# Splitting the second layer's first expert weights on ScalarE and GpSimd instead of VectorE

## The reference

```python
x = x + tanh(g_xattn[0]) * L0_xattn(layernorm(x), ctx)
x = x + tanh(g_ffn[0])   * L0_ffn(layernorm(x))
x = x + tanh(g_xattn[1]) * L1_xattn(layernorm(x), ctx, mask)
x = x + tanh(g_ffn[1])   * L1_ffn(layernorm(x))
# L1_ffn: the token rows are sorted by expert, cut into 8 equal chunks, and chunk e is worked by expert e
h = gelu(einsum('ecd,edf->ecf', chunks, w1)); y = einsum('ecf,efd->ecd', h, w2)
```

## Time and profile before

| | |
|---|---|
| median of three runs | 760.68 us (760.11 to 762.44) |
| profiled execution | 758.21 us, its span 756.4 us |
| mean granted PE clock of the profiled execution | 0.827 |
| busy in the span | PE 545.8, DVE 416.9, POOL 339.5, ACT 237.2 us |

### The profile page before, as it was taken

The page is one execution under the profiler, slowest core; times in us unless marked ns, Lnnn a source line. Parts: engine busy times, 40 slices in busy tenths (PEclk is TensorE's granted clock), DMA queues, the critical chain, the costliest instruction groups (busy, mean ns, idle before and its releaser), DMA issues.

```text
span 756.4 us, 17521 instructions
## 1 busy us (share of the span) xinstructions
PE 545.8 (72%) x5484; PEld 428.4 (57%) x5485; DVE 416.9 (55%) x1454; ACT 237.2 (31%) x415; POOL 339.5 (45%) x424
## 2 busy tenths in 40 slices
PE   1576755524799999991898897777871388999950
PEld 1333443401499899980454575666651166989950
DVE  4787697986033333334995377778568612222215
ACT  0321022121144444443422364554541021323210
POOL 6202107777255666666400000070747676666650
PEclk9886867656899999996689899696655599999985
DMA  7911001143132222343754264352324123322219
GB/s 205 270 36 43 29 1 53 51 136 109 50 81 79 75 82 73 81 130 120 210 169 142 54 179 123 109 161 50 71 63 131 46 55 101 85 78 77 71 58 311
DMA packets 73196, 76.54 MB, mean 101 GB/s; under 512 B 12984, under 2 KB 61368, under 8 KB 73064
## 3 DMA queue, kind: packets, MB, share of 16 engines
q1 hardware_dynamic: 58504, 50.98, 24.6%
q0 software_dynamic: 10224, 22.40, 9.5%
q10 hardware_dynamic: 4400, 2.26, 1.0%
HBM read 46.15 MB, written 29.34 MB: 100 GB/s over the span
## 4 chain that ended last, share of the span: by engine, by line
PE 51%; DVE 23%; POOL 8%; issue 8%; DMA 6%; ACT 1%; SPq 1%; POOLq 0%; DVEq 0%
PE PS L758 46%; POOL xs L517 5%; DMA work<-ys 3%; DVE stats L1331 3%; DVE XN L1352 2%; PE PS L947 2%; DVE X L1326 2%; DVE work L1741 2%; DVE work L1326 2%; DVE rtmp L1326 1%; POOL work L565 1%; DVE mv L1334 1%; PE PS L1097 1%; DVE nwt L1326 1%; POOL work L572 1%
## 5 line engine op out<-in xcount | busy, mean ns | idle before, releaser
L517 POOL DMA_INDIRECT xs<-pack,adr_i x80 | 78.0, 975 | 196.7 <-ACT pack L1172 141.1
L528 POOL DMA_INDIRECT ys<-work x144 | 140.7, 977 | 34.5 <-issue 34.5
L758 PE MATMUL PS<-w,work 128*128 x1152 | 144.3, 279 | 3.0 <-issue 2.2
L758 PEld LDWEIGHTS PS<-w,work 128*128 128x128 f32 x1152 | 135.3, 193 | 9.2 <-issue 7.1
L758 PE MATMUL PS<-work,w1h 128*128 128x256 f16 x576 | 99.8, 275 | 2.6 <-issue 1.3
L1224 ACT ACTIVATE work<-PS,b 128x256 f32<-128x256 f32 x160 | 62.6, 474 | 95.4 <-PE PS L758 95.4
L1326 DVE TENSOR_TENSOR work<-PS,work 128x256 f32<-128x256 f32 (+3 forms) x82 | 33.0, 404 | 94.4 <-issue 52.9
L758 PE MATMUL PS<-work,w1l 128*128 128x256 f16 x288 | 79.4, 276 | 0.0
L758 PE MATMUL PS<-work 97*64 97x256 f16 (+5 forms) x608 | 61.3, 316 | 16.2 <-DVE work L1458 9.4
L758 PE MATMUL PS<-ones 128*128 128x512 f16 x195 | 51.9, 426 | 27.8 <-DVE rows_i L1588 12.6
L1661 DVE TENSOR_SCALAR work<-PS,work 128x128 f32<-128x128 f32 x64 | 19.5, 346 | 79.1 <-PE PS L758 79.1
(11 more groups left out here) (262 smaller groups left out, 852.5 us busy)
## 6 DMA issues: line engine op xcount, KB each, us to landing
work<-xs SPq DMA_DIRECT2D x132, 65.0 KB
work<-ys SPq DMA_DIRECT2D x12, 512.0 KB, 6.0
k_parts<-work SPq DMA_DIRECT2D x24, 128.0 KB, 2.0
w<-k_parts SPq DMA_DIRECT2D x8, 384.0 KB
work<-k_parts SPq DMA_DIRECT2D x32, 96.0 KB
work<-q_parts SPq DMA_DIRECT2D x8, 384.0 KB
work<-q_parts SPq DMA_DIRECT2D x32, 96.0 KB
ys<-work POOLq DMA_INDIRECT x144
```

Of the source, the lines that this page charges most:

```text
L517: g.indirect_dma_start(xs[l], bass.IndirectOffsetOnAxis(adr_i[:, k, T:T + 1], 0), pack_of(l, c)[:, s, k, :].bitcast(U32), None)\
L528: g.indirect_dma_start(ys[l], bass.IndirectOffsetOnAxis(xin[:, q, u, :].bitcast(U32)[:, D:D + 1], 0), yrow[:, q, u, :], None).then_inc(ff[ ...
L758: return t.matmul(o, lhsT, rhs, start=start, stop=stop, skip_group_check=True)
```

## The change

VectorE's splits of the second layer are taken out. In the same iterations 3, 7, ... 31, ScalarE, behind its copy of the turned heads and ahead of its routing steps, scales the loaded weights in place (f32 to f32), waits for that, and copies them to float16 as the high part. GpSimd subtracts the high from the scaled weights: for experts 0 to 3 ahead of all scatters, for 4 and 5 ahead of chunk 2's scatters, for 6 and 7 ahead of chunk 4's. The waits that stood before the first split (the stores of the queries, which share the memory of `w1h` and `w1l`) move to ScalarE with it.

```diff
--- before.py
+++ after.py
@@ -291,6 +291,7 @@
         w2_in = sem("w2_in")
         pack_hi, pack_lo = sem("pack_hi"), sem("pack_lo")
         w1_lo = [sem(f"w1_lo{l}") for l in range(2)]
+        w1_scaled, w1_hi = sem("w1_scaled"), sem("w1_hi")
 
         ff = {k: [sem(f"f_{k}{u}") for u in range(n)] for k, n in
               (("xin", XS_LEAD), ("xT", 2), ("xT_sb", 2), ("up", 2), ("hid", 2), ("y", 2), ("yrow", 2), ("turn", 1),
@@ -549,7 +550,17 @@
                 rows, s_, value = y_slot(0, c)
                 pool.wait_ge(s_, value)
                 g.tensor_tensor(rows[:, :, 0, :], rows[:, :, 0, :], rows[:, :, 1, :], ALU.add).then_inc(y_sum, 1)
+            def low_w1(e):
+                pool.wait_ge(w1_hi, e + 1)
+                o = slice(e * FF, (e + 1) * FF)
+                g.tensor_tensor(w1l[:, o], w1raw1[:, e % 2, :], w1h[:, o], ALU.subtract).then_inc(w1_lo[1], 1)
+
+            for e in range(E // 2):
+                low_w1(e)
             for c in range(NC):
+                if c in (2, 4):
+                    for e in (E // 2 + c - 2, E // 2 + c - 1):
+                        low_w1(e)
                 if c < NC // 2:
                     for s in range(CT_TILES):
                         scatter(1, c, (s,))
@@ -1300,6 +1311,15 @@
                         act.wait_ge(q_blank, 1)
                         act.wait_ge(n_out, 32)
                         max_loaded(act, 0)
+                k = chunk_at(g, 3)
+                if k == 0:
+                    for c in range(NC):
+                        act.wait_ge(q_out[c], Q_STORED)
+                if k is not None:
+                    act.wait_ge(w1_in[1][k % 2], 16 * (k // 2 + 1))
+                    a.activation(w1raw1[:, k % 2, :], w1raw1[:, k % 2, :], ACT.Copy, scale=WSCALE).then_inc(w1_scaled, 1)
+                    act.wait_ge(w1_scaled, k + 1)
+                    a.activation(w1h[:, k * FF:(k + 1) * FF], w1raw1[:, k % 2, :], ACT.Copy).then_inc(w1_hi, 1)
                 for k in route_at("exp", g):
                     route_exp(1, k)
                 for c in route_at("high", g):
@@ -1762,12 +1782,6 @@
                     route_weights(1, k)
                 for c in route_at("pack", g):
                     route_pack(1, c)
-                k = chunk_at(g, 3)
-                if k == 0:
-                    for c in range(NC):
-                        dve.wait_ge(q_out[c], Q_STORED)
-                if k is not None:
-                    split_w1(1, w1raw1, k)
             route_table(1)
             experts(1)
             for c in range(NC):
```

## The result

The changed kernel took 765.88 us (median of 20 runs, 761.02 to 772.62) against 757.86 us (20 runs, 752.13 to 763.93) for the kernel before on the same chip: a ratio of 1.0104, with a 95% interval of 1.0079 to 1.0129. The forecast was +7.9 us, 1.0%.

What follows compares the result with a forecast made beforehand. GpSimd's scatter queue was taken to set the end from 559.93 us, the PE/VectorE loop before. Terms -2.1 + 1.5 + 3.3 and +5.2 gave +7.9: 766.1, with 2.5 carried over 768.6 us; range 763.4 to 771.0.

Steps and rivals of the forecast that it cites:

- partial port waits: Band of 763 to 767 us, where VectorE is held by GpSimd only in part; chance 0.27.
- the 2.5 us carried over: Earlier median of 760.68 us lies 2.5 above the profiled execution of 758.21; added to 766.1 to give 768.6.
- Queue on GpSimd, +5.2: Eighth subtraction, waiting for ScalarE, delays chunk 4's first of 32 back-to-back scatters: +5.2 us, bounds 4.8 and 6.0.
- VectorE's port, +3.3: GpSimd's subtractions 3, 4 and 5 hold VectorE's routing instructions at the shared SBUF port, 3 x 1.1 us; bounds 0 and 4.8.
- Number 4: GpSimd subtraction, counted from 0, behind chunk 1's last scatter: holds VectorE 1.1 us, felt at PE's 0.70 us wait at 514.71.
- number 6: GpSimd subtraction, counted from 0, on VectorE's normalisation at 550: no cost, 3.40 us of VectorE idle behind it.
- ScalarE's stalls, +1.5: ScalarE's pair delays PE after iterations 3 (+0.9 us) and 7 (+0.6), nothing elsewhere; bounds 0 and 4.
- VectorE's relief, -2.1: Splits removed from VectorE count only after iterations 15 and 23, 2 x 1.06 us; PE's clock 0 to 2.0 more, taken as 0.
- Rival 1: VectorE's port is not felt, routing instructions slip between: +4.6 us, 765.3 us; with partial port waits chance 0.27.
- Rival 2: VectorE's relief counts in full and PE's clock holds, no ScalarE stall or port wait: +1.1 us, 761.8 us; chance 0.07.
- Rival 3: VectorE's routing, not GpSimd's scatters, ends last, so the delay is absorbed: faster, 756.6 to 758.6 us; chance 0.06.
- Rival 4: Eighth subtraction is not waited for, only the loop's +2.7 us is left: 763.4 us; given no chance of its own.

Runs made afterwards that it cites:

- experiment 2: Changed kernel with the eighth split whole back on VectorE: 759.55 us, 1.0027 to the kernel before.
- experiment 4: Changed kernel with GpSimd's subtractions 3, 4 and 5 (counted from 0) each later, behind scatters of the next chunk: 761.50 us, 1.0047 to the kernel before.
- experiment 6: Changed kernel with subtractions 3, 4, 5 later behind scatters and the eighth split back on VectorE: 755.35 us, 0.9956 to the kernel before.
- Experiment 5: Changed kernel with the splits of experts 0 and 1 back on VectorE: 765.56 us, 1.0104 to the kernel before.
- Experiment 8: Kernel before with VectorE's splits of experts 3 and 5 moved from iterations 15 and 23 to 18 and 26, still on VectorE: 752.91 us, 0.9932.
- experiment 1: Changed kernel with the eighth ScalarE split ahead of iteration 31's heads' copy instead of behind it: 764.37 us, 1.0077 to the kernel before.
- experiment 3: Changed kernel with GpSimd's subtractions 3, 4 and 5 (counted from 0) each done twice in a row: 765.35 us, 1.0116 to the kernel before.

## Why the prediction was right

The sign and the difference came out as forecast: +1.04% for +1.0%, +8.0 us by the medians for +7.9. The level didn't. 765.88 us lies 2.7 below 768.6, in the band that the prediction gave to partial port waits, because the three runs it started from stand high: the kernel before has a median of 757.86 us in twenty runs, not 760.68. Without the 2.5 us carried over for it the forecast was 766.1.

That the sum agrees to 0.1 us is in part luck. Taking away the queue saves 5.8 us (experiment 2), the holds 4.3 (experiment 4), both together 1.0104 - 0.9956, 11.2 us (experiment 6), where the forecast had 5.2 + 3.3 = 8.5; and what is then left of the change is -3.3 us, where the forecast had -2.1 + 1.5 = -0.6. By these values the costs were forecast too small and the relief too small, and the two errors cancel. Each of the differences is good to some 3 us, so the direction is surer than the sizes. By its steps:

- **Queue on GpSimd, +5.2**: right. 4.93 at the first scatter, 5.18 at the second; 5.8 us by experiment 2. The pair took 1.28 us from 568.86 to the end at 570.14 (1.30 forecast) and the subtraction 1.15 (1.27). What I didn't see is a gap of 0.54 us instead of 0.30 ahead of the second scatter.
- **VectorE's port, +3.3**: right in place, and in size for the holds it counted, 3.0 us under subtractions 3, 4 and 5. Number 4 reached PE at another wait than the one it named: 1.05 us at 517.68, while the 0.70 us that the earlier trace rows has at 514.71 stayed 0.70. It missed number 6: the normalisation was held for 1.7 us. The 3.40 us of VectorE's idle time don't stand directly behind it, the heads for PE's next step come first, and PE waited 0.51 us. It also priced a hold without the clock behind PE's longer wait: 4.3 us by experiment 4. The reductions beside other subtractions keep their time: one at 435.25 took 1.22 us beside subtraction 0, the mean of all 32 by the page is 1.223. The reads from PSUM, of which the prediction had no row, keep theirs too: in experiment 4 the addition at 532.95, beside a subtraction at 532.66, takes 0.29 us, as it does with none beside it. The Trainium skill, GPSIMD Engine Reference, section 8 "Key points", names two SBUF operands or a two-port mode as what collides. The count has two SBUF operands; the TENSOR_SCALAR of 1.24 us, the CAST of 1.92 us and the normalisation read one tensor, so they would have to come under the second half of the rule, and no row here shows a mode; the measured holds decide.
- **ScalarE's stalls, +1.5**: shown in the rows, not in the time. The pair costs 1.29 us in iteration 3 (434.54 to 435.83, forecast 1.30) and the transpose behind it stands 0.84 us (0.9). In iteration 7 of this execution PE waited for a transfer in any case; executions without that wait show 0.48 us (0.6). Experiment 5 found no time in either, so whether they reach the end is open.
- **VectorE's relief, -2.1, with 0 to 2.0 more for the clock**: the most mis-sized term. In the changed kernel it is right that nothing is left over: the hold fills the gap, and PE waits 3.06 us. But the forecast had written relief and hold as separate terms that add up (-2.1 and +3.3), and had bounded the clock by an average over twenty iterations (0.73 against 1.0). The rows of the places show five steps at half speed behind each wait, 1.5 and 1.6 us, so that the two are worth 5.3 us where the clock follows; the outer bound was -2.1 - 2.0 = -4.1. Experiment 8's time, 5.2 us with an interval from 2.7 to 7.7, doesn't exclude that bound.
- **The rivals.** Rival 1 (port not felt) falls by the rows of 1.15 to 1.24 us and by experiment 4. Rival 2 (relief in full, clock kept) is not what the changed kernel did; experiments 4 and 6 to 8 had the relief at both places, and the clock with it in full at six of the eight. Rival 3 falls by experiment 2: the 5 us given back to the queue came off the end. Rival 4 falls by the subtraction at 570.22.

The profiled execution put PE's wait at 646.77 where I had said near 642; 4.8 us, the difference, is also what this execution lies above its median.

## What to carry to other kernels

Before an instruction is moved to an idle engine, look at what stands behind it in that engine's queue: one subtraction of 1.15 us ahead of 32 back-to-back scatters cost 5 to 6 us, because it waited for a third engine. GpSimd's elementwise work is not free to VectorE: in most collisions seen here an instruction of 0.2 us took about as long as GpSimd's or longer, so such work belongs beside reductions, not beside short routing steps that PE waits for. And where only two of eight splits lay on the path, moving these two by three iterations on their own engine gave more than handing all eight away.

## What the runs showed of the hardware that was not expected

- A VectorE instruction with one SBUF input is held beside GpSimd's elementwise instruction too: a TENSOR_SCALAR of 128x64 1.24 us for 0.19, in experiment 1 a COPY of 128x8 1.14 for 0.17 (at 566.47). Not each one: a RECIPROCAL of 128x8 kept its 0.20 us inside a subtraction (experiment 3).
- The hold can be longer than the subtraction. The CAST of 128x64 in experiment 4 took 1.92 us for 0.20, begun 0.70 us ahead of a subtraction of 1.15 us; in experiment 2 a product of 128x64, begun at 511.63, 0.64 us ahead, took 1.89 for 0.23. Both ended within 0.1 us of the subtraction. Why a hold reaches back ahead of it stays open.
- PE's clock mostly follows the length of the wait at the two places: 0.66 us for 16 matmuls, the upper level, behind 2.07 us, and 1.07, the lower, behind 3.06. It is not the length of the wait alone: in the changed kernel a wait of 2.09 us at 474.50 was followed by 16 matmuls in 1.07 us, and there PE had run the steps from 467.89 to 470.75 at the lower level; and the 2.07 us in experiment 6 above were followed by 1.07 after steps at the upper level. What decides it stays open.
